# Experts' second product in three float32r terms, its high weights fetched tile by tile by GpSimd, and some steps moved around it

## What is computed

```python
scores = xf @ gate_w.T
ew, ei = jax.lax.top_k(scores, TOP_K)
ew = jax.nn.softmax(ew, axis=-1)
x1 = jax.nn.silu(jnp.einsum('td,ehd->teh', xf, w_gate))
x3 = jnp.einsum('td,ehd->teh', xf, w_up)
expert_out = jnp.einsum('teh,edh->ted', x1 * x3, w_down)
onehot = jax.nn.one_hot(ei, N_EXPERTS, dtype=ew.dtype)
comb = jnp.einsum('ta,tae->te', ew, onehot)
routed = jnp.einsum('te,ted->td', comb, expert_out)
shared = jax.nn.silu(xf @ sh_gate.T) * (xf @ sh_up.T) @ sh_down.T
sgate = jax.nn.sigmoid(xf @ se_gate_w.T)
return (routed + sgate * shared).reshape(Bb, Tt, Cc)
...
x = _layernorm(x + _L0_attn_ref(...), axis=-1)
x = _layernorm(x + _L0_ffn_ref(...), axis=-1)
```

## Time and profile before

| | |
|---|---|
| median of 3 runs | 2044.42 us (2044.05 to 2047.7) |
| profiled execution | 2047.9 us |
| its span, first to last instruction | 2046.2 us |
| PE busy | 1971.2 us (96%) |
| DVE busy | 1344.6 us (66%) |
| ACT busy | 888.2 us (43%) |
| POOL busy | 942.9 us (46%) |
| granted TensorE clock, mean | 0.989 |

### The profile page before, as it was taken

The page is one execution under the profiler, slowest core; times in us unless marked ns, Lnnn a source line. Parts: engine busy times, 40 slices in busy tenths (PEclk is TensorE's granted clock), DMA queues, the critical chain, the costliest instruction groups (busy, mean ns, idle before and its releaser), DMA issues.

```text
span 2046.2 us, 31314 instructions
## 1 busy us (share of the span) xinstructions
PE 1971.2 (96%) x10048; PEld 1280.0 (63%) x10049; DVE 1344.6 (66%) x2296; ACT 888.2 (43%) x1571; POOL 942.9 (46%) x893
## 2 busy tenths in 40 slices
PE   7999999999999999999999998879999999999997
PEld 5655555755555755555755545568766666667886
DVE  5777776678777677777477776579233444446865
ACT  2366664366665366665266565311111111112322
POOL 3255654455665455665355556549111111114651
PEclk9999999999999999999999999989999999999999
DMA  7312433403432503432503323775643332347752
GB/s 231 73 41 70 99 79 93 140 23 85 102 79 71 162 17 82 99 92 54 170 27 69 68 74 104 260 303 181 249 170 103 102 97 98 103 168 228 224 174 71
DMA packets 103699, 242.11 MB, mean 118 GB/s; under 512 B 25296, under 2 KB 25808, under 8 KB 98576
## 3 DMA queue, kind: packets, MB, share of 16 engines
q1 hardware_dynamic: 92768, 205.06, 33.1%
q0 software_dynamic: 10800, 35.40, 6.2%
HBM read 132.93 MB, written 56.61 MB: 93 GB/s over the span
## 4 chain that ended last, share of the span: by engine, by line
PE 86%; DVE 4%; DMA 3%; SPq 3%; issue 2%; ACT 1%; POOL 1%; ACTq 0%; DVEq 0%; POOLq 0%
PE ps_gu L1698 18%; PE ps_s L723 11%; PE ps_side L701 11%; PE ps_ctx L734 10%; PE ps_side L675 9%; PE ps_d L1804 6%; PE ps_sum L747 5%; PE ps_d L1698 4%; PE ps_t L1769 1%; SPq L359 1%; PE ps_side L667 1%; DMA inv_rows<-inv_few 1%; DMA x_r<-x 1%; PE ps_side L772 1%; PE ps_side L769 1%
## 5 line engine op out<-in xcount | busy, mean ns | idle before, releaser
L1002 DVE TENSOR_REDUCE max_half<-ps_side 128x1 f32<-128x512 f32 x1024 | 658.8, 682 | 211.7 <-PE ps_side L701 208.5
L701 PE MATMUL ps_side<-kq_stack 96*128 96x512 f32 x1024 | 409.3, 404 | 4.9 <-DVE max_half L1002 2.3
L723 PE MATMUL ps_s<-kq_stack 97*128 97x512 f32 x937 | 392.2, 419 | 8.3 <-ACT probs_first L887 4.6
L723 PEld LDWEIGHTS ps_s<-kq_stack 97*128 97x128 f32 x937 | 177.4, 189 | 165.4 <-issue 85.5
L887 ACT ACTIVATE probs_first<-ps_s 128x512 f32<-128x512 f32 x326 | 187.7, 600 | 101.1 <-PE ps_s L723 85.5
L701 PEld LDWEIGHTS ps_side<-kq_stack 96*128 96x128 f32 x1024 | 195.5, 191 | 57.0 <-DVE max_half L1002 25.5
L887 ACT ACTIVATE probs_mid<-ps_s 128x512 f32<-128x512 f32 x308 | 177.5, 599 | 111.9 <-PE ps_s L723 97.3
L622 POOL TENSOR_TENSOR acc<-probs_first,probs_mid 128x512 f32<-128x512 f32 x129 | 163.8, 1296 | 131.1 <-ACT probs_mid L887 131.1
L887 ACT ACTIVATE probs_last<-ps_s 128x512 f32<-128x512 f32 x303 | 175.8, 599 | 99.2 <-PE ps_s L723 83.2
L622 POOL TENSOR_TENSOR acc<-probs_last,probs_first 128x512 f32<-128x512 f32 x129 | 163.3, 1292 | 117.6 <-ACT probs_first L887 117.6
L1653 POOL DMA_INDIRECT x_g<-x,who_all x71 | 67.4, 949 | 323.4 <-PE ps_t L1769 315.5
(11 more groups left out here) (252 smaller groups left out, 3674.2 us busy)
## 6 DMA issues: line engine op xcount, KB each, us to landing
kq_stack<-kq SPq DMA_DIRECT2D x192, 256.0 KB, 5.1
y_slots<-y_t SPq DMA_DIRECT2D x71, 256.0 KB, 2.3
x_r<-x SPq DMA_DIRECT2D x32, 256.0 KB, 3.9
x_t<-x SPq DMA_DIRECT2D x32, 256.0 KB, 4.1
gu_sb<-wgu SPq DMA_DIRECT2D x8, 1024.0 KB, 15.4
gu_kept<-gu_part SPq DMA_DIRECT2D x32, 256.0 KB, 2.4
...
```

The lines of the kernel that those rows point to most:

```text
L701: nc.tensor.matmul(bank, q_stack[par][0:3 * HD, h, t * P:(t + 1) * P], k_stack[par][0:3 * HD, h, half * HALF:(half + 1) * HALF], start=Tru ...
L723: nc.tensor.matmul(out, k_stack[par][0:3 * HD + 1, h, kt * P:(kt + 1) * P], q_stack[par][0:3 * HD + 1, h, half * HALF:(half + 1) * HALF], ...
L1002: nc.vector.reduce_max(max_half[:, u // 2, u % 2:u % 2 + 1], bank, AX.X).then_inc(side_free, 1)
```

## The change

- **Attention**: in the last group of the last batch, six of the eight `row_sums` come two score products later (`sums_later`).
- **Scores**: the router's high and low weights stand side by side as 32 columns, so a group takes 8 products instead of 12; the two halves of the result are added by the transposing product (`twice`). The cover's first tile is turned ahead of the last group's scores (`FirstTile`).
- **Slot places**: `positions` is cut in two, `positions` after tile 2 and `places` after tile 3; column counts, table parts, look-ups and `who` come one tile later each.
- **Split of weights**: the experts' second weights are split too, 16 parts more on POOL (48 in all), with a buffer `wd_lo` on chip and `wd_kept` in DRAM. After part 41 POOL issues the first four gathers. The load of the first `gu_hi` needs all 48 parts stored, and only half of `up(11)`.
- **Experts**: `expert_down` is six float32r products. Its high weights (512 KB) are loaded for every tile by POOL's queue into `wd_hi[t % 2]`: POOL waits for `expert_down(t - 2)`, reads the expert's number, issues the load of tile t, and then the gather of tile t + 3. The hidden values get a high half (ACT) and a low half (DVE) instead of one DVE copy. `expert_turn(t + 1)` stands ahead of `expert_up(t)`. The last `expert_down` is inside `up(12)`.
- Buffers move: `wd_hi[1]` lies over the half of `x_t` for tiles 14 and 15, so SP loads these two tiles late, at slot tile 69.

```diff
+def sums_later(last, loc):
+
+
+    return last and loc >= (G - 1) * STEPS and loc % FOLD == FOLD - 1 and loc % KT != KT - 1
...
-                            row_sums(b, loc)
+                            if not sums_later(last, loc):
+                                row_sums(b, loc)
+                        if slot == SUMS_LATER and loc and sums_later(last, loc - 1):
+                            row_sums(b, loc - 1)
...
-                    xh, xl = xT_hi[:, g, c, :], xT_lo[:, g, c, :]
-                    for i, (w, m) in enumerate(((rw_hi, xh), (rw_lo, xh), (rw_hi, xl))):
-                        done = nc.tensor.matmul(ps_s[0:RW, g, :], w[:, c, :], m, start=c == 0 and i == 0,
-                                                stop=c == C - 1 and i == 2)
+                    for i, x in enumerate((xT_hi, xT_lo)):
+                        done = nc.tensor.matmul(ps_s[0:2 * RW, g, :], rw_parts[:, c].rearrange("p a n -> p (a n)"),
+                                                x[:, g, c, :], start=c == 0 and i == 0, stop=c == C - 1 and i == 1)
...
+class FirstTile:
+
+
...
+    def turn(self, pe):
+        m = self.memory
+        pe.wait_ge(self.router.t_hi, TT - 3)
+        pe.wait_ge(self.router.t_lo, TT - 3)
+        pe.wait_ge(self.router.x_in[0], 16 * (TT // 4 + 1))
+        for c in range(C):
+            done = self.nc.tensor.transpose(m.ps_t[:, 0, c * P:(c + 1) * P], m.x_t[:, 0, c * P:(c + 1) * P], self.ident[:])
+        done.then_inc(self.t_ready, 1)
...
+                if last:
+                    first_tile.turn(pe)
                 score(q, g)
                 if not first:
...
-COUNT_COLUMNS_AFTER = 3
-TABLE_AFTER = {3: (0, 1), 4: (2, 3), 5: (4, 5), 6: (6, 7)}
-LOOK_UP_AFTER = {4: (0, 1), 5: (2, 3), 6: (4, 5), 7: (6, 7)}
-WHO_AFTER = 7
+COUNT_COLUMNS_AFTER = 4
+TABLE_AFTER = {4: (0, 1), 5: (2, 3), 6: (4, 5), 7: (6, 7)}
+LOOK_UP_AFTER = {5: (0, 1), 6: (2, 3), 7: (4, 5), 8: (6, 7)}
+WHO_AFTER = 8
+GATHER_AFTER = 40
+PARTS = E * C + E * CH
 PARTS_FIRST = 3
...
             for i in range(2):
-                sp.wait_ge(part_out[i], 16 * (E * C // 2))
-            sp.wait_ge(router.st_split, 3 * C + E * C)
+                sp.wait_ge(part_out[i], 16 * (PARTS // 2))
+            sp.wait_ge(router.st_split, 3 * C + PARTS)
             sp.wait_ge(shared_kept, 16 * KEPT_PIECES)
-            sp.wait_ge(gu_ready, COVER)
+            sp.wait_ge(half_up, 1)
             sp.sem_inc(passed, 1)
             load_high(0)
+            sp.wait_ge(gu_ready, COVER)
             load_high(1)
             store_base(COVER - 2)
-            load_tile(COVER + 2)
             for e in range(2):
                 high_landed(e)
                 load_high(e + 2)
             store_base(COVER - 1)
-            load_tile(COVER + 3)
             sp.wait_ge(d_ready, COVER)
             for e in range(2, 4):
                 high_landed(e)
...
+                if t == NT - 2:
+                    load_tile(COVER + 2)
+                    load_tile(COVER + 3)
...
+            for i in range(PARTS):
+                if i < E * C:
+                    raw, low = [w[:, i // C, i % C, :] for w in (gu_sb, gu_lo)]
+                else:
+                    raw, low = [w[:, (i - E * C) // CH, i % CH, :] for w in (wd_sb, wd_lo)]
...
+                if i == GATHER_AFTER:
+                    pool.wait_ge(placed, 2)
+                    pool.sem_inc(passed, 1)
+                    for t in range(4):
+                        gather_x(t)
             for t in range(NT):
-                if t >= 4:
-                    pool.wait_ge(et_ready, t - 3)
+                if t < 2:
+                    pool.wait_ge((ht_ready, base_done)[t], COVER)
+                    for i in range(2):
+                        pool.wait_ge(part_out[i], 16 * (PARTS // 2))
+                else:
+                    pool.wait_ge(ey_ready, t - 1)
+                pool.sem_inc(passed, 1)
+                e = pool.value_load(tile_expert[0:1, t:t + 1], min_val=0, max_val=E - 1)
+                nc.gpsimd.dma_start(wd_hi[t % 2][:].bitcast(F32), wd_kept[bass.ds(e, 1)].rearrange("a p c d -> (a p) c d")).then_inc(
+                    wd_hi_in[t % 2], 16)
+                if t and t + 3 < NT:
+                    pool.wait_ge(et_ready, t)
                     pool.sem_inc(passed, 1)
-                nc.gpsimd.indirect_dma_start(
-                    x_g[:, t % 4, :], None, x2, bass.IndirectOffsetOnAxis(ap=who_all[:, t:t + 1].bitcast(U32), axis=0),
-                ).then_inc(xg_in[t % 4], 16)
+                    gather_x(t + 3)
...
+                by_chunk = t == COVER - 1
+                for k, c in sorted(itertools.product(range(2), range(C)), key=lambda kc: kc[1] if by_chunk else kc[0]):
+                    done = three(ps_gu[:, k, :], (xT_hi[:, t % 2, c, :], xT_lo[:, t % 2, c, :]),
+                                 (sgu_hi[:, c, k, :], sgu_lo[:, c, k, :]), c, C - 1)
+                    if by_chunk and (k, c) == (1, C // 2 - 1):
+                        done.then_inc(half_up, 1)
...
                 pe.wait_ge(eht_done, t + 1)
+                pe.wait_ge(eht_low, t + 1)
+                pe.wait_ge(wd_hi_in[s % 2], wd_loads(t, s))
                 if not static(t, 2):
                     pe.wait_ge(ey_done, t - 1)
                 elif t == 0:
                     pe.wait_ge(base_done, COVER)
                 for c in range(CH):
-                    done = nc.tensor.matmul(ps_d[:, s % 2, :], e_hT[:, s % 2, c, :],
-                                            wd_sb[:, bass.ds(e, 1), c, :].rearrange("p a n -> p (a n)"),
-                                            start=c == 0, stop=c == CH - 1)
+                    low = wd_lo[:, bass.ds(e, 1), c, :].rearrange("p a n -> p (a n)")
+                    done = three(ps_d[:, s % 2, :], (e_hT_hi[:, s % 2, c, :], e_hT_lo[:, s % 2, c, :]),
+                                 (wd_hi[s % 2][:, c, :], low), c, CH - 1)
                 done.then_inc(ey_ready, 1)
...
             def expert_step(t, s):
+                if not static(t, 1) and not is_last(t):
+                    expert_turn(t + 1, (s + 1) % 4)
                 expert_up(t, s, expert_of(t))
-                if not is_last(t):
-                    expert_turn(t + 1, (s + 1) % 4)
+                if is_last(t):
+                    turn(COVER)
                 if not static(t, 1):
                     expert_down(t - 1, (s - 1) % 4, expert_of(t - 1))
                 expert_turn_hidden(t, s)
 
...
-            expert_turn(0, 0)
+            for t in range(2):
+                expert_turn(t, t)
             down(COVER - 1)
-            pe.wait_ge(wd_in, 16 * E)
-            pe.wait_ge(router.st_split, 3 * C + E * C)
-            pe.wait_ge(expert_known, 1)
+            pe.wait_ge(router.st_split, 3 * C + PARTS)
+            pe.wait_ge(placed, 1)
             expert_pipeline(pe, expert_step, lambda: pe.wait_ge(hi_known, E))
-            turn(COVER)
-            expert_down(NT - 1, (NT - 1) % 4, expert_of(NT - 1))
-
             for t in range(COVER, TT):
-                up(t)
+                if t == COVER:
+                    up(t, lambda: expert_down(NT - 1, (NT - 1) % 4, expert_of(NT - 1)))
+                else:
+                    up(t)
                 if t < TT - 1:
...
+            def expert_h_high(t, s):
+                act.wait_ge(eht_ready, t + 1)
+                if not static(t, 2):
+                    act.wait_ge(ey_ready, t - 1)
+                nc.scalar.activation(e_hT_hi[:, s % 2], ps_hts[:, s % 2, 0:H].rearrange("p (c t) -> p c t", c=CH),
+                                     ACT.Copy).then_inc(eht_done, 1)
+
...
-            def expert_h_copy(t, s):
-                dve.wait_ge(eht_ready, t + 1)
+            def expert_h_low(t, s):
+                dve.wait_ge(eht_done, t + 1)
                 if not static(t, 2):
                     dve.wait_ge(ey_ready, t - 1)
-                nc.vector.tensor_copy(e_hT[:, s % 2], ps_hts[:, s % 2, 0:H].rearrange("p (c t) -> p c t", c=CH)).then_inc(eht_done, 1)
+                nc.vector.tensor_tensor(e_hT_lo[:, s % 2], ps_hts[:, s % 2, 0:H].rearrange("p (c t) -> p c t", c=CH),
+                                        e_hT_hi[:, s % 2].bitcast(F32), ALU.subtract).then_inc(eht_low, 1)
 
...
             def expert_step(t, s):
+                if not static(t, 1) and not is_last(t):
+                    expert_x_low(t + 1, (s + 1) % 4)
                 expert_hidden(t, s)
-                if not is_last(t):
-                    expert_x_low(t + 1, (s + 1) % 4)
+                if is_last(t):
+                    x_low(COVER)
                 if not static(t, 1):
                     expert_y_copy(t - 1, (s - 1) % 4)
-                expert_h_copy(t, s)
+                expert_h_low(t, s)
 
...
+                return end
+
+            def places(end):
+                shift = P.bit_length() - 1
...
                 elif t == 1:
                     running = count()
                 elif t == 2:
```

(6 more changed lines are left out.)

195 lines of the change are left out of this document (117 added, 78 removed).

## The result

The changed kernel takes 2072.7 us (median of 4 runs, 2072.08 to 2076.39) against 2044.66: 1.0138 times the time before, 95% interval 1.012 to 1.0155. It is slower by 28 us, where 2030 was predicted. The profiled execution spans 2069.6 us against 2046.2: 23.4 us are to be explained. (Between the medians it is 28, mostly because the profiled execution of before is 3.2 us above its median. Of this 2.1 us lie ahead of any changed instruction: the last denominators before the changed ones come at 1206.78 now and at 1208.93 before.)

What follows compares the result with a forecast made beforehand. TensorE's list, in its order, was taken as the time. Terms +2.3 (start of tile 4), -18.1 (67 tiles), +2.0 (`wd_hi` waits), -1.0 (the end) gave -14.8 us, so 2030 from the median; range 2023 to 2037, 2014 to 2046 for 8 in 10.

Steps and rivals of the forecast that it cites:

- Second product: Expert tiles 4 to 70: six float32r products replace the float32 product, saving 0.27 us a tile, 18.1 us in all.
- rival 3: Expert loop: TensorE's own queue bounds, the expert-number read sits in the open, gain 0.10 a tile, 2041 us; chance 0.08.
- Start of tile 4: Passage from cover to experts: tile 4 counts as starting at 1500.5, 2.3 us later than in the kernel before.
- `wd_hi` hidden: Expert tiles: the 512 KB load per tile is hidden with 2.5 us to spare; 2.0 us of waits in the last tiles.
- Cover: Tiles before the experts: TensorE would end them some 19 us sooner, at 1454 instead of 1473.
- the denominators: Late attention: waits of 0.86 us partly filled by moving them later, 3.0 us earlier, bounds 0 and 5.
- the scores: Router scores before the experts: 32 products less, 5 us for TensorE and 3.3 us for the last transposes.
- the seam: Passage from cover to experts: all gained in attention, scores and cover would be lost waiting there for loads.
- The end: Last expert tile: `expert_down(70)` inside `up(12)` fills a wait; 1 us gained for the first `up`, nothing for the rest.

Runs made afterwards that it cites:

- experiment 3: Changed kernel with x turned after the first product again, on TensorE, ScalarE and VectorE: 2059.9 us, 1.0077 of before.
- Experiments 1 and 2: Changed kernel with the read of the expert's number moved ahead of the hidden transposes: 2040.8 us; changed kernel with four second products instead of six: 2068.3 us.
- experiment 7: Changed kernel with the expert-number read ahead of the hidden transposes and `gu_hi` loads 0 to 5 issued between the last parts' stores: 2034.8 us, 0.9945 of before.
- experiment 8: experiment 7 with the experts' second product as before, plain float32, without `wd_hi` and `wd_lo`: 2025.2 us, 0.9899 of before.
- Experiment 5: Changed kernel with the last two stores of shared weights (`sd_hi`, `sd_lo`) issued two cover tiles sooner: 2068.0 us, 1.0115 of before.
- experiment 10: Changed kernel with the expert-number read ahead of the hidden transposes, and `wd_hi` loaded for tiles 0 and 1 only: 2029.2 us, 0.9919 of before.
- Experiment 11: Changed kernel with only the experts' second product as before, plain float32, no parts of wd, no `wd_hi`: 2041.2 us, 0.9977 of before.

## Why the prediction was wrong

- **Second product, -18.1 us.** This term failed. Each product does cost 0.23 us and the six 1.40 (1.46 predicted), but I took the saving off the tile as if the tile were the sum of the array's work. I checked that the hidden product is ready before the second product ends, with 0.4 us left, and stopped at that point. Behind it stand, in TensorE's queue, the issue of six transposes, the read and its register work, 1.25 us until the next product: 1.03 + 1.25 = 2.28, where the array is busy for 1.40 + 0.22 + 0.35 = 1.97. I even credited 0.01 us for turning x ahead of the first product, where experiment 3 shows that this very move costs 13 us in the whole. The queue was rival 3, with a chance of 0.08 and 0.10 us of gain left; the tile came out 0.09 longer. Experiments 1 and 2 show it: the read ahead takes 0.53 us off a tile, a third fewer products nothing. With the read out of the way the six products save 0.33 a tile (4.80 in experiment 7, 5.13 in experiment 8) where I had 0.27: the array's side of the term was sound.
- **Start of tile 4, +2.3.** It came 7.8 us later for the first product. POOL's last part ends at 1464.3 instead of 1461.3. The larger miss is SyncE: I took the first load as issued when the last part has landed, 1462.6. In the list, behind the last parts, stand the stores of `sd_hi`, of a finished tile, a load of x and the store of `sd_lo`, 1 MB, and the load waits for that to land: 1472.23. Experiment 5, with the last two stores sooner, gets 4.3 us of this back. I had followed POOL's list item by item, and SyncE's not; the trace of the kernel before had the same wait, 4.6 us. From the first load to tile 4 I said 36.1, it was 33.7, and the two waits of TensorE, said to be 13 and 9 us, were 15.8 and 4.0.
- **`wd_hi` hidden, +2.0 in the last tiles.** Hidden in the loop, as predicted, with landing at 4.0 us for 4.5 assumed (experiment 10). In the last tiles the term was mis-sized: 5.0 us of waits and 6.8 in all, in the stretch in which SyncE loads the shared weights; experiment 10 shows that it goes with the loads of `wd_hi`.
- **Cover.** Right in kind, and smaller: the wait of 9.82 is 1.38, the last hidden transposes of the cover come 14.4 us sooner (1454.12 against 1468.51), but TensorE ends the cover at 1462.9, 10.7 us sooner, and not at 1454, 19 sooner. Ahead of `down(11)` it stands for 2.89 us, and the first seven products after that start some 0.43 us apart. That costs nothing here, since TensorE waits for `gu_hi` behind it. The `gu_sb` loads go out at 1314.67 (1314.5 predicted), in part by luck: of the 6.1 us, 2.1 are there before anything changed, the denominators give 2.7 (3.0 predicted; the last come at 1253.16 against 1258.03), and only 1.3 are left for the scores (3.3 predicted). That the gain would be lost at the seam was right as well. Experiment 11 shows that it is lost with the 16 parts: without them (and without the six products and their loads, which come later) the first `gu_hi` load is issued 19 us sooner.
- **The end, -1.0.** It gives 0.6. The last store's 2.6 us were not foreseen; they are there in every trace with a load of `wd_hi` for each tile and in none without (experiment 10), and I can't say why.

The sum by the same terms: 8.6 + 5.2 + 6.8 - 0.6 + 3.4 = 23.4, where I had -14.8. In the 8.6 there are 1.6 us of clock that I had foreseen with 1.8: after the wait the first eight products of tile 4 are 0.43 us apart instead of 0.23, and the stretch 1500 to 1520 has a granted clock of 0.91.
